# The expert stage of an attention and mixture-of-experts kernel with its tile loops written out

## The chip, the cores and the metric

The kernel runs on one core of a Trainium2 chip. The metric is the device time of one execution in microseconds (us). The engines are named as in the profile: PE (TensorE, matrix products), ACT (ScalarE), DVE (VectorE), POOL (GpSimd), SP (SyncE, which here only issues DMAs). Each engine runs its own instruction stream and meets the others only through semaphores.

## The reference, cut to what matters

The inputs are `x` and a context, each 128 sequences of 64 tokens of 128 numbers, 8192 tokens in all.

```python
x = x + xattn(layernorm(x), ctx, ctx)      # 16 heads of 64, causal, projected by Wo
z = layernorm(layernorm(x)) * ln_g + ln_b
w = top-2 of softmax(z @ rW + rb), renormalised          # 8 experts
hid = gelu(z @ W1[e] + b1[e])                            # 128 -> 256
mixed = sum over e of w[e] * (hid @ W2[e] + b2[e])       # 256 -> 128
return x + layernorm(x) + mixed
```

Each token goes to its two best experts only.

## The kernel before

**The attention stage**, up to about 754 us of the profiled execution, works through 16 groups of 512 tokens. PE, ACT, DVE, POOL and SP each run a hardware loop over groups. While it does group g it also routes the tokens of group g-1: DVE works out each token's two experts and a slot in the region of each, and POOL scatters the normalised rows to `slots` in DRAM by indirect DMA.

**The expert stage**, from about 754 to 1024 us, works through NT = 71 tiles of 256 slots. All slots of a tile belong to one expert, and which one is known only at run time: SP and DVE read the tile's row and expert from SBUF into a register (`value_load`). Buffers are DEEP = 4 deep, PSUM banks 2 deep. For one tile the engines do this:

- SP (`next_tile`, `load_tile`, lines 432 to 454): waits until tile s-4 has been transposed and its destinations are worked out, reads the row number, loads 256 rows of `slots` into `zin` (in the trace `kf<-slots`).
- PE (`rows_t` L1143, `up` L908 to L912, `down` L1161 and L1166): transposes tile s, multiplies tile s-1 by W1, tile s-2 by W2.
- ACT (`hi_part` L846, `results` L861, `hidden` L853): copies out the transposed rows of tile s, copies out the results of tile s-3 (`y_sb`, in the trace `kf<-bank`), applies Gelu to tile s-1.
- DVE (`lo_part` L1569, `expert_of` L1554, `places` L1586, `weights` L1560 to L1562, `destinations` L1575 and L1578): the low part of tile s, the indices `ix_i` to which the results of tile s-3 go, the weights of the expert of tile s+1 and its destinations.
- POOL (L704): two indirect DMAs for each tile scatter its results to `mixed` in DRAM. It waits for `ix_i` and `y_sb`, and its stream over all 71 tiles is written out in both kernels. The buffers `y_sb` and `ix_i` of tile s are free again when the scatters of tile s-4 have landed (`out_s`).

In the streams of the other four engines some of the tiles are written out one by one, and some are done in a loop whose body holds 4 tiles (SP, PE) or 8 (ACT, DVE). In a loop the tile's number is in a register, and a wait for a count that grows with the tile is a wait for a register's value, worked out by register instructions ahead of it. The loop's head is aligned (`head_slot`).

| engine | written out | in a loop | written out |
|---|---|---|---|
| SP | 0 to 23, 32 to 35 | 24 to 31 and 36 to 47 (2 and 3 rounds) | 48 to 70 |
| PE | 0 to 23 | 24 to 67 (11 rounds of 4) | 68 to 70 |
| ACT | 0 to 23 | 24 to 47 (3 rounds of 8) | 48 to 70 |
| DVE | 0 to 23 | 24 to 47 (3 rounds of 8) | 48 to 70 |

Beside tiles 0 to 23 stand the last group's routing and tables (DVE, PE, ACT), eight DMAs that pad the regions (`pad`, SP, L432 and L433, after tile 16), and beside tiles 54 to 70 the first ten groups are read back from `mixed`, scaled and added to `x` (`load_y`, `scale_second`, `add_experts`, `store`). The last six groups follow after the last tile.

Of the kernel before, what the change touches and what calls it, by code (L numbers as in the profile page):

```python
# [106 lines left out]
def xattn_ffn_kernel(nc, x, ctx_in, mask, Wq, Wk, Wv, Wo, bo, ln_g, ln_b, rW, rb, W1, b1, W2, b2, out):  # L107
# [8 lines left out]
    NG = NP // GP  # L116
# [4 lines left out]
    FG = 10  # L121
# [4 lines left out]
    FULL = -(-(2 * FG * TG - SPILL) // TILE)  # L126
# [11 lines left out]
    with ExitStack() as es:  # L138
# [116 lines left out]
        DEEP = 4  # L255
# [92 lines left out]
        def aligned_loop(engine, first, end):  # L348

            return nc.Fori(first, end, engines=[engine], head_slot={engine: 0})  # L350

        ROUTE = 23
        STRAIGHT = 24
        LOOPED = 48
        ADD_AT = dict(zip((54, 56, 58, 60, 62, 64, 66, 68, 69, 70), range(FG)))
        assert DONE <= LOOPED and len(ADD_AT) == FG and NT == 71

        def by_seq(par, b):
            return pr[par][:, :, :].rearrange("p (j b) s -> p j b s", b=2)[:, :, b, :]
# [26 lines left out]
        def _(sp):  # L386
# [54 lines left out]
            def rest_ready():  # L441

                sp.wait_ge(pad_ok, 16 * (1 + E))
                sp.wait_ge(sent, 32 * GP * NG)
                sp.wait_ge(tab, TAB_ALL)
# [6 lines left out]
            def next_tile(s, buf):  # L452
                sp.wait_ge(ct_ps, s - DEEP + 1)
                sp.wait_ge(yi_st, 2 * (s - DEEP) + 2)
                load_tile(s, buf)
# [17 lines left out]
            sp.wait_ge(sc_ps, 2 * (NP - 2))  # L473
            for s in range(DEEP):
                load_tile(s, s)
            for s in range(DEEP, STRAIGHT):
                next_tile(s, s % DEEP)
                if s == 16:
                    pad()
            with aligned_loop(mybir.EngineType.SP, STRAIGHT // DEEP, FULL // DEEP) as ss:  # L480
                for buf in range(DEEP):
                    next_tile(DEEP * ss + buf, buf)
            for s in range(FULL // DEEP * DEEP, FULL):
                next_tile(s, s % DEEP)
            rest_ready()
            for s in range(FULL, -(-FULL // DEEP) * DEEP):
                next_tile(s, s % DEEP)
            with aligned_loop(mybir.EngineType.SP, -(-FULL // DEEP), LOOPED // DEEP) as ss:
                for buf in range(DEEP):
                    next_tile(DEEP * ss + buf, buf)  # L490
            loaded = added = 0
            for s in range(LOOPED, NT):
                next_tile(s, s % DEEP)
                if s - 1 in ADD_AT:
                    if loaded == 0:
                        mixed_ready(DONE)
                    load_y(loaded)
                    loaded += 1
                if s - 5 in ADD_AT:
                    store(added)  # L500
                    added += 1
# [208 lines left out]
        def _(act):  # L710
# [131 lines left out]
            def hi_part(s, deep):  # L842
                act.wait_ge(ct_ps, s + 1)
                if not isinstance(s, int) or s >= DEEP:
                    act.wait_ge(up_ps, s - DEEP + 1)
                act.activation(z_hi[deep], bank[deep % 2][:, 0:TILE], ACT.Copy).then_inc(ch_hi, 1)  # L846

            def hidden(s, deep):
                act.wait_ge(up_ps, s + 1)
                if not isinstance(s, int) or s >= DEEP:  # L850
                    act.wait_ge(dn_ps, s - DEEP + 1)
                for c in range(FC):
                    act.activation(hid[deep][:, c, :], bank[2 + deep % 2][:, c * TILE:(c + 1) * TILE], ACT.Gelu,  # L853
                                   bias=w_f[deep][:, B1 + c:B1 + c + 1]).then_inc(gl_ok, 1)

            def results(s, deep):

                act.wait_ge(dn_ps, s + 1)
                if not isinstance(s, int) or s >= DEEP:
                    act.wait_ge(out_s[deep], 4 * TJ * (s - deep))  # L860
                act.activation(y_sb[deep], bank[4 + deep % 2][:, 0:TJ * D].rearrange("p (j d) -> p j d", d=D),  # L861
                               ACT.Copy).then_inc(yv_ok, 1)
# [13 lines left out]
                if s >= 1:  # L876
                    hidden(s - 1, (s - 1) % DEEP)

            for s in range(STRAIGHT):
                tile_out(s)  # L880
                if s == 4:
                    act.wait_ge(rz_ps, 1)
                    act.activation(z2T[:, :], bank[6][:, :], ACT.Copy).then_inc(rz_ok, 1)
                if s == 7:
                    r_exp(NG - 1)
            with aligned_loop(mybir.EngineType.Activation, STRAIGHT // (2 * DEEP), LOOPED // (2 * DEEP)) as ss:
                for k in range(2 * DEEP):
                    hi_part(2 * DEEP * ss + k, k % DEEP)
                    results(2 * DEEP * ss + k - 3, (k - 3) % DEEP)
                    hidden(2 * DEEP * ss + k - 1, (k - 1) % DEEP)  # L890
            act.wait_ge(rt_ok, ROUTE * NG)
            for s in range(LOOPED, NT):
                tile_out(s)
                if s in ADD_AT:
                    scale_second(ADD_AT[s])
            results(NT - 3, (NT - 3) % DEEP)
# [8 lines left out]
        def _(pe):  # L905
# [270 lines left out]
            rows_t(0, 0)  # L1176
            rows_t(1, 1)
            up(0, 0)
            for s in range(2, STRAIGHT):
                tile_products(s)  # L1180
                if s == 4:
                    pe.wait_ge(shifted, 2 * NP)
                    pe.wait_ge(zn_ok, GP * NG)
                    turned_rows(bank[6], zlast).then_inc(rz_ps, 1)
                if s == 5:
                    pe.wait_ge(att_ok, NP)
                    pe.wait_ge(rz_ok, 1)
                    logits(bank[7]).then_inc(rl_ps, 1)
                if s == 8:
                    pe.wait_ge(ch_ok, NG)  # L1190
                    ranks(bank[6]).then_inc(rx_ps, 1)
            with aligned_loop(mybir.EngineType.PE, STRAIGHT // DEEP, NT // DEEP) as ss:
                for k in range(DEEP):
                    rows_t(DEEP * ss + k, k)
                    up(DEEP * ss + k - 1, (k - 1) % DEEP)
                    down(DEEP * ss + k - 2, (k - 2) % DEEP)
            for s in range(NT // DEEP * DEEP, NT):
                tile_products(s)
            up(NT - 1, (NT - 1) % DEEP)
            down(NT - 2, (NT - 2) % DEEP)  # L1200
            down(NT - 1, (NT - 1) % DEEP)
# [3 lines left out]
        def _(dve):  # L1205
# [414 lines left out]
            weights(1, 1, expert_of(1))  # L1620
            add_attention(NP - 1)
            destinations(0, 0)
            for s in range(STRAIGHT):
                tile_in(s, s)
                if s == 0:
                    dve.wait_ge(att_ok, NP)
                    norm_stats(lambda t: xs[:, (NG - 1) * GP + t, :], norm[1], s1_ok, NG - 1)
                    twice_normed(NG - 1)
                if s == 1:
                    route_b(NG - 2)  # L1630
                if s == 2:
                    last_rows()
                if s == 6:
                    dve.wait_ge(rl_ps, 1)
                    route_a(NG - 1, bank[7], rl_ok, 1, zlast, first=True)
                if s == 9:
                    dve.wait_ge(rx_ps, 1)
                    route_c(NG - 1, bank[6], rx_ok, slot_ix_last)
                    dve.wait_ge(rx_ok, 1)
                    step(dve.tensor_copy(next_i[:, :], next_slot[:, :]))  # L1640
                    assert count[0] == TAB_NEXT
                if s == 10:
                    tiles_up(n_ceil[:, :], next_slot, 0)
                if s == 11:
                    step(dve.tensor_tensor(runs[:, 2, :], n_ceil[:, :], run_from[:, 2, :], ALU.subtract))
                    run_ends(2, 1)
                if s == 12:
                    later_ends()
                    step(dve.memset(run_row[:, RUNS:RUNS + 1], float(DEAD)))
                if s == 13:  # L1650
                    run_rows(1, 2)
                    run_jumps(RUNS)
                if s == 14:
                    route_b(NG - 1)
                if s == 15:
                    past_runs(REST, RUNS)
                if s == 16:
                    jumped_rows(REST, RUNS)
                if s == 18:
                    tile_experts(REST)  # L1660
                    assert count[0] == TAB_ALL
            with aligned_loop(mybir.EngineType.DVE, STRAIGHT // (2 * DEEP), LOOPED // (2 * DEEP)) as ss:
                for k in range(2 * DEEP):
                    tile_in(2 * DEEP * ss + k, k)
            dve.wait_ge(base_ok, NG)
            for s in range(LOOPED, NT):
                if s < NT - 1:
                    tile_in(s, s)
                else:
                    lo_part(s, s % DEEP)  # L1670
                    places(s - 3, (s - 3) % DEEP)
                if s in ADD_AT:
                    add_experts(ADD_AT[s])
# [31 lines left out]
```

## Time and profile before

| what | value |
|---|---|
| time, median of 3 runs | 1052.81 us (1048.83 to 1059.91) |
| the profiled execution | 1052.08 us |
| its span, first to last instruction | 1050.3 us |
| mean granted TensorE clock | 0.936 of full speed |
| busy: PE, DVE, ACT, POOL | 86%, 70%, 58%, 47% of the span |

The span is what the rows of the trace add up to; the 1.8 us between it and the execution's time lie before the first and after the last instruction. Shares are averages over stages: in the expert stage alone no engine is as busy as PE is in the attention stage. "Idle before" a row is the time in which its engine did nothing ahead of it, with who ended that. "Issue" means that the profile shows nothing that the engine waited for, and "remote", "another core or an unknown queue" that what released it came from none of the engines in the profile.

### The profile page before, as it was taken

The page shows a single profiled execution, that of the slowest core. Times are in us where ns is not written, and L with a number is a line of the kernel's source. Part 1 is how long each engine was busy: PE and PEld are TensorE (multiplying, and loading weights), DVE is VectorE, ACT ScalarE, POOL GpSimd, SP SyncE. Part 2 cuts the span into 40 slices and gives each one's busy share as a digit, 9 for nine tenths or more (in the row PEclk, how much of TensorE's full clock was granted, in tenths as well). Part 3 has the DMA queues.
Part 4 walks back from the last instruction along what each step waited for, and adds up shares of the span by engine and source line. Part 5 has one row for each costly group of instructions (what it writes and reads, how often), then busy time and mean ns, then how long its engine had stood idle before and what let it go on. Part 6 is the DMA issues. An engine that isn't in the chain of part 4 may idle for free.

```text
span 1050.3 us, 36518 instructions
## 1 busy us (share of the span) xinstructions
PE 900.1 (86%) x13368; PEld 784.9 (75%) x13368; DVE 731.1 (70%) x2239; ACT 611.7 (58%) x1317; POOL 489.0 (47%) x601
## 2 busy tenths in 40 slices
PE   8998999999999999999999999997776677777670
PEld 6887888887888888888888888886665566666560
DVE  6787877777777777777778787679366543445664
ACT  6675766766676676667567566665343343335462
POOL 2833543436454353644436364323356644555551
PEclk9999999999999999999999999999699678888895
DMA  9001010101001010110101000001123222224655
GB/s 283 20 22 31 15 35 8 35 8 38 29 11 35 5 35 11 34 30 10 36 5 35 28 18 23 8 17 28 36 62 103 81 75 69 72 80 138 190 164 197
DMA packets 55664, 56.63 MB, mean 54 GB/s; under 512 B 7335, under 2 KB 48593, under 8 KB 55601
## 3 DMA queue, kind: packets, MB, share of 16 engines
q1 hardware_dynamic: 46651, 37.94, 12.7%
q0 software_dynamic: 8640, 17.84, 5.1%
q8 instruction: 30, 0.49, 0.2%
q14 instruction: 33, 0.27, 0.1%
q10 hardware_dynamic: 310, 0.08, 0.1%
HBM read 32.62 MB, written 23.23 MB: 53 GB/s over the span
## 4 chain that ended last, share of the span: by engine, by line
PE 72%; issue 9%; another core or an unknown queue 6%; ACT 5%; DVE 4%; DMA 2%; SPq 1%; POOL 0%; DVEq 0%; ACTq 0%; POOLq 0%
PE bank L1023 11%; PE bank L908 10%; PE bank L912 10%; PE bank L909 9%; PE bank L1039 9%; PE bank L1008 7%; PE bank L991 5%; PE bank L1166 4%; ACT pr L853 2%; PE bank L961 1%; PE bank L936 1%; PE bank L1143 1%; DMA kf<-mixed 1%; PE bank L939 1%
## 5 line engine op out<-in xcount | busy, mean ns | idle before, releaser
L908 PE MATMUL bank<-in_h,Ah 128*128 128x256 f32 x654 | 212.6, 325 | 29.3 <-DVE Al L1569 16.3
L775 ACT ACTIVATE pr<-pr 128x512 f32<-128x512 f32 x128 | 80.4, 628 | 233.7 <-DVE pr L1281 233.7
L704 POOL DMA_INDIRECT mixed<-kf,ix_i x142 | 139.0, 979 | 115.7 <-DVE ix_i L1586 71.0
L728 ACT ACTIVATE kf<-bank 128x512 f32<-128x512 f32 x256 | 156.5, 612 | 8.0 <-PE bank L912 4.6
L908 PEld LDWEIGHTS bank<-in_h,Ah 128*128 128x128 f32 x654 | 128.6, 197 | 39.5 <-DVE Al L1569 19.0
L912 PE MATMUL bank<-in_h,Al 128*128 128x256 f32 x512 | 145.0, 283 | 0.0
L909 PE MATMUL bank<-in_l,Ah 128*128 128x256 f32 x512 | 144.6, 282 | 0.0
L615 POOL DMA_INDIRECT slots<-zrow,slot_ix x120 | 125.6, 1046 | 37.9 <-issue 28.3
L1279 DVE TENSOR_REDUCE mx<-bank 128x8 f32<-128x512 f32 x128 | 87.8, 686 | 76.0 <-PE bank L1039 75.8
L1023 PE MATMUL bank<-wo_s,oT 128*128 128x128 f32 x1024 | 134.8, 286 | 2.3 <-ACT oT L770 2.3
L550 POOL TENSOR_TENSOR idle_p<-half 128x1 f32<-128x1 f32 x114 | 27.5, 241 | 227.9 <-DVE slot_ix L1372 186.9
L1039 PEld LDWEIGHTS bank<-kf 64*64 64x64 f32 x4096 | 82.7, 136 | 66.8 <-issue 65.7
L1039 PE MATMUL bank<-kf 64*64 64x64 f32 x4096 | 103.4, 227 | 31.2 <-issue 30.1
L1166 PE MATMUL bank<-kf,pr 128*128 128x128 f32 x568 | 95.7, 319 | 39.2 <-ACT pr L853 35.1
L1023 PEld LDWEIGHTS bank<-wo_s,oT 128*128 128x128 f32 x1024 | 122.4, 196 | 6.9 <-ACT oT L770 2.7
L1291 DVE TENSOR_TENSOR pr<-pr,ri 128x512 f32<-128x512 f32 x128 | 115.4, 902 | 4.4
L1166 PEld LDWEIGHTS bank<-kf,pr 128*128 128x128 f32 x568 | 81.0, 220 | 50.0 <-ACT pr L853 37.5
L853 ACT ACTIVATE pr<-bank,kf 128x256 f32<-128x256 f32 x142 | 59.8, 477 | 76.5 <-remote 53.2
L555 POOL TENSOR_TENSOR rs<-ve,half 128x4 f32<-128x4 f32 (+1 forms) x32 | 43.7, 1366 | 125.7 <-DVE ve L1220 100.4
L909 PEld LDWEIGHTS bank<-in_l,Ah 128*128 128x128 f32 x512 | 98.0, 191 | 0.0
L912 PEld LDWEIGHTS bank<-in_h,Al 128*128 128x128 f32 x512 | 97.2, 190 | 0.0
L1281 DVE TENSOR_TENSOR pr<-bank,mx 128x512 f32<-128x512 f32 x128 | 88.5, 692 | 4.4
(191 smaller groups left out, 1955.6 us busy)
## 6 DMA issues: line engine op xcount, KB each, us to landing
kf<-slots SPq DMA_DIRECT2D x71, 130.0 KB
kf<-mixed SPq DMA_DIRECT2D x12, 512.0 KB
xs<-in_x_dram SPq DMA_DIRECT2D x16, 256.0 KB
c_in<-in_ctx_dram SPq DMA_DIRECT2D x16, 256.0 KB
out_dram<-xs SPq DMA_DIRECT2D x16, 256.0 KB
mixed<-kf,ix_i POOLq DMA_INDIRECT x142
vf<-mixed SPq DMA_DIRECT2D x4, 512.0 KB
slots<-zrow,slot_ix POOLq DMA_INDIRECT x120
```

The costliest lines, as they stand in the source:

```text
L615: pool.indirect_dma_start(out=slots, out_offset=bass.IndirectOffsetOnAxis(ap=ix[:, k, t:t + 1], axis=0), in_=rows[:, t, :], in_offset=None ...
L704: pool.indirect_dma_start(out=mixed, out_offset=bass.IndirectOffsetOnAxis(ap=ix_i[buf][:, j:j + 1], axis=0), in_=y_sb[buf][:, j, :], in_of ...
L728: act.activation(kfs[par][:, 2 * u:2 * u + 2, :], ring[gr.bank(name)].rearrange("p (h t) -> p h t", h=2), ACT.Copy).then_inc(act_ev, 1)
L908: pe.matmul(ps, lh, rh, start=True, stop=False)
L909: pe.matmul(ps, lh, rl, start=False, stop=False)
L912: return pe.matmul(ps, ll, rh, start=False, stop=True)
L1023: last = pe.matmul(o_ps[:, 0:D], oT[:, j, :], wo_s[:, j, :], start=(j == 0), stop=(j == H // 2 - 1))
L1039: last = pe.matmul(s_ps[b][place, S * j:S * j + S], kfs[par][dims, j, toks], kfs[par][dims, H // 2 + j, toks], start=False, stop=True, ski ...
L1166: last = pe.matmul(into[:, j, :], hid[deep][:, c, j * P:(j + 1) * P], w_f[deep][:, c * D:(c + 1) * D], start=False, stop=(c == FC - 1), sk ...
L1279: dve.reduce_max(mx[:, par, hs], src, AX_X).then_inc(sm_st, 1)
L1281: dve.tensor_tensor(by_seq(par, t), src, mx[:, par, hs].unsqueeze(2).to_broadcast([P, 8, S]), ALU.subtract).then_inc(shifted, 1)
L1291: dve.tensor_tensor(by_seq(par, t), by_seq(par, t), ri[:, par, hs].unsqueeze(2).to_broadcast([P, 8, S]), ALU.mult).then_inc(probs, 1)
```

## The change

The loops are gone. On SP, PE, ACT and DVE each tile from 24 on is written out as the first 24 and the last 23 were: the tile's number is a constant, each wait is for a constant, and buffer addresses are constants. The row and the expert of a tile are still read from SBUF into a register by each of SP and DVE. The order of the work on each engine is the same, with two places where it is now a condition in one long loop of the program text: `rest_ready` on SP still comes ahead of tile 33, and ACT's wait for `rt_ok` still comes after tile 47, now behind the work of tile 48 instead of ahead of it. PE's whole stream of 71 tiles is written out, DVE waits for `base_ok` ahead of tile 48 as before. The attention stage's loops stay.

```diff
@@ SP
-            for s in range(DEEP, STRAIGHT):
+            for s in range(DEEP, ADD_FROM):
+                if s == FULL:
+                    rest_ready()
                 next_tile(s, s % DEEP)
                 if s == 16:
                     pad()
-            with aligned_loop(mybir.EngineType.SP, STRAIGHT // DEEP, FULL // DEEP) as ss:
-                for buf in range(DEEP):
-                    next_tile(DEEP * ss + buf, buf)
...
-            with aligned_loop(mybir.EngineType.SP, -(-FULL // DEEP), LOOPED // DEEP) as ss:
-                for buf in range(DEEP):
-                    next_tile(DEEP * ss + buf, buf)
@@ ACT
-            for s in range(STRAIGHT):
+            for s in range(NT):
                 tile_out(s)
...
-            with aligned_loop(mybir.EngineType.Activation, STRAIGHT // (2 * DEEP), LOOPED // (2 * DEEP)) as ss:
-                for k in range(2 * DEEP):
-                    hi_part(2 * DEEP * ss + k, k % DEEP)
-                    results(2 * DEEP * ss + k - 3, (k - 3) % DEEP)
-                    hidden(2 * DEEP * ss + k - 1, (k - 1) % DEEP)
-            act.wait_ge(rt_ok, ROUTE * NG)
-            for s in range(LOOPED, NT):
-                tile_out(s)
+                if s == ADD_FROM:
+                    act.wait_ge(rt_ok, ROUTE * NG)
@@ PE
-            for s in range(2, STRAIGHT):
+            for s in range(2, NT):
                 tile_products(s)
...
-            with aligned_loop(mybir.EngineType.PE, STRAIGHT // DEEP, NT // DEEP) as ss:
-                for k in range(DEEP):
-                    rows_t(DEEP * ss + k, k)
-                    up(DEEP * ss + k - 1, (k - 1) % DEEP)
-                    down(DEEP * ss + k - 2, (k - 2) % DEEP)
@@ DVE
-            for s in range(STRAIGHT):
+            for s in range(ADD_FROM):
                 tile_in(s, s)
...
-            with aligned_loop(mybir.EngineType.DVE, STRAIGHT // (2 * DEEP), LOOPED // (2 * DEEP)) as ss:
-                for k in range(2 * DEEP):
-                    tile_in(2 * DEEP * ss + k, k)
```

## Rows read from the trace of the kernel before

**Rows 1.** Busy time by stretch; columns: the stretch, then each engine, PEclk the granted clock.
```profile
core 0: us, PE busy (x) PEld busy (x) DVE busy (x) ACT busy (x) POOL busy (x), PEclk, DMA share, GB/s
849.00:935.00 86.00, 65.25 (x408) 56.50 (x407) 38.51 (x161) 32.65 (x92) 45.31 (x47) 0.84 0.25 73
935.00:957.00 22.00, 16.88 (x103) 14.57 (x102) 9.94 (x44) 9.81 (x28) 10.25 (x11) 0.84 0.30 91
```
**Rows 2.** Timeline of ACT, start and length in us: `hi_part` of tiles 17, 24, 48, 54, 70.
```profile
825.62 0.38 ACT L846 ACTIVATE in_h<-bank 128x256 fp32r<-128x256 f32 x1
...
850.88 0.38 ACT L846 ACTIVATE in_h<-bank 128x256 fp32r<-128x256 f32 x1 [2.67 <-PE bank L912]
...
936.69 0.40 ACT L846 ACTIVATE in_h<-bank 128x256 fp32r<-128x256 f32 x1
...
957.58 0.38 ACT L846 ACTIVATE in_h<-bank 128x256 fp32r<-128x256 f32 x1 [0.68 <-PE bank L1143]
...
1018.79 0.38 ACT L846 ACTIVATE in_h<-bank 128x256 fp32r<-128x256 f32 x1 [2.51 <-remote]
```
**Rows 3.** Groups by line, busy and idle before: 850.8 to 936.6 us, then 936.6 to 957.5.
```profile
L846 ACT ACTIVATE in_h<-bank 128x256 fp32r<-128x256 f32 x24 | 9.3, 387 | 22.3 <-PE bank L1143 7.8 <-PE bank L912 5.6 <-issue 4.5
...
L846 ACT ACTIVATE in_h<-bank 128x256 fp32r<-128x256 f32 x6 | 2.3, 390 | 5.5 <-remote 2.6 <-PE bank L1143 1.7 <-issue 1.2
```
**Rows 4.** Timeline of POOL, looped tiles: a run of six scatters and the next run's first.
```profile
893.81 0.97 POOL L704 DMA_INDIRECT mixed<-kf,ix_i  x1 [2.65 <-DVE ix_i L1586]
...
900.14 0.96 POOL L704 DMA_INDIRECT mixed<-kf,ix_i  x1 [0.30 <-issue]
904.99 0.97 POOL L704 DMA_INDIRECT mixed<-kf,ix_i  x1 [3.90 <-DVE ix_i L1586]
```
**Rows 5.** Timeline of ACT beside that run.
```profile
896.21 0.38 ACT L861 ACTIVATE kf<-bank 128x256 f32<-128x256 f32 x1
902.43 0.84 ACT L853 ACTIVATE pr<-bank,kf 128x256 f32<-128x256 f32 x2 [5.84 <-remote]
```
**Rows 6.** Timeline of POOL and ACT, written-out tiles: first and last scatter of a run of six.
```profile
987.73 0.96 POOL L704 DMA_INDIRECT mixed<-kf,ix_i  x1 [1.66 <-DVE ix_i L1586]
...
994.33 0.96 POOL L704 DMA_INDIRECT mixed<-kf,ix_i  x1 [0.30 <-issue]
...
990.36 0.39 ACT L861 ACTIVATE kf<-bank 128x256 f32<-128x256 f32 x1
996.42 0.84 ACT L853 ACTIVATE pr<-bank,kf 128x256 f32<-128x256 f32 x2 [5.67 <-remote]
```
**Rows 7.** Waits, 849 to 935 us (loops): total us, times, longest.
```profile
POOL mixed L704 <- DVE ix_i L1586: 28.6, 10, 3.9
...
ACT pr L853 <- remote: 22.1, 5, 5.8
...
DVE ix_i L1586 <- issue: 11.7, 23, 0.8
```
**Rows 8.** Waits, 935 to 957 us (written out but for PE).
```profile
ACT pr L853 <- remote: 4.7, 1, 4.7
...
DVE ix_i L1586 <- issue: 2.3, 7, 0.5
```
**Rows 9.** Instruction packets (count, MB): 797 to 849 us, then 851 to 935.
```profile
q8 instruction: 2, 0.03, 0.3%
q14 instruction: 5, 0.04, 0.2%
...
q14 instruction: 3, 0.02, 0.1%
```
**Rows 10.** Waits of PE over the whole span: a wait in the attention stage.
```profile
PE bank L936 <- issue: 3.5, 4, 2.9
```
**Rows 11.** The chain that ended last, 790 to 812 us: start, us, what.
```profile
796.40 0.71 SPq L432
...
797.86 0.70 SPq L433
```

More of the change, by code:

```diff
@@ L352, in xattn_ffn_kernel @@
         ROUTE = 23
-        STRAIGHT = 24
-        LOOPED = 48
+        ADD_FROM = 48
         ADD_AT = dict(zip((54, 56, 58, 60, 62, 64, 66, 68, 69, 70), range(FG)))
-        assert DONE <= LOOPED and len(ADD_AT) == FG and NT == 71
+        assert DONE <= ADD_FROM and len(ADD_AT) == FG and NT == 71
         def by_seq(par, b):
@@ L479, in _ @@
                     pad()
-            with aligned_loop(mybir.EngineType.SP, STRAIGHT // DEEP, FULL // DEEP) as ss:
-                for buf in range(DEEP):
-                    next_tile(DEEP * ss + buf, buf)
[L483 to L487, printed above, removed]
-            with aligned_loop(mybir.EngineType.SP, -(-FULL // DEEP), LOOPED // DEEP) as ss:
-                for buf in range(DEEP):
-                    next_tile(DEEP * ss + buf, buf)
             loaded = added = 0
-            for s in range(LOOPED, NT):
+            for s in range(ADD_FROM, NT):
                 next_tile(s, s % DEEP)
@@ L885, in _ @@
                     r_exp(NG - 1)
-            with aligned_loop(mybir.EngineType.Activation, STRAIGHT // (2 * DEEP), LOOPED // (2 * DEEP)) as ss:
-                for k in range(2 * DEEP):
-                    hi_part(2 * DEEP * ss + k, k % DEEP)
-                    results(2 * DEEP * ss + k - 3, (k - 3) % DEEP)
-                    hidden(2 * DEEP * ss + k - 1, (k - 1) % DEEP)
-            act.wait_ge(rt_ok, ROUTE * NG)
-            for s in range(LOOPED, NT):
-                tile_out(s)
+                if s == ADD_FROM:
+                    act.wait_ge(rt_ok, ROUTE * NG)
                 if s in ADD_AT:
@@ L1191, in _ @@
                     ranks(bank[6]).then_inc(rx_ps, 1)
-            with aligned_loop(mybir.EngineType.PE, STRAIGHT // DEEP, NT // DEEP) as ss:
-                for k in range(DEEP):
-                    rows_t(DEEP * ss + k, k)
-                    up(DEEP * ss + k - 1, (k - 1) % DEEP)
-                    down(DEEP * ss + k - 2, (k - 2) % DEEP)
-            for s in range(NT // DEEP * DEEP, NT):
-                tile_products(s)
             up(NT - 1, (NT - 1) % DEEP)
@@ L1661, in _ @@
                     assert count[0] == TAB_ALL
-            with aligned_loop(mybir.EngineType.DVE, STRAIGHT // (2 * DEEP), LOOPED // (2 * DEEP)) as ss:
-                for k in range(2 * DEEP):
-                    tile_in(2 * DEEP * ss + k, k)
             dve.wait_ge(base_ok, NG)
-            for s in range(LOOPED, NT):
+            for s in range(ADD_FROM, NT):
                 if s < NT - 1:
```

## The prediction

> **What bounds the kernel now.** I read the busy time by stretch first, to see whether an engine fills the part that the change touches. None does: over the looped tiles PE is busy 65.25 of 86 us, POOL 45.31, DVE 38.51, ACT 32.65, and over the first tiles behind the loops PE has 16.88 of 22 us, much the same share [rows 1]. So the stage is bounded by waits, and the next view is the timeline, for the pace. Tile 24 to tile 48 is 936.69 - 850.88 = 85.81 us for 24 tiles, 3.58 us a tile [rows 2, 3]. PE, the busiest engine, has 65.25 / 24 = 2.7 us of work in each, with a mean granted clock of 0.84 [rows 1], so 0.9 us or more of every tile is waiting.
>
> Where does it wait? POOL's timeline shows it. POOL works in runs: six scatters back to back from 893.81 to 901.10, one every 1.27 us, which is 2.53 us a tile, then nothing until 904.99 [rows 4]. ACT stops inside such a run: its last copy ends at 896.59, 2.8 us after the run's start, and the next Gelu starts at 902.43, 1.3 us after the run's end, released by something "remote" [rows 5]. PE then has no Gelu output, and DVE no high part. Once ACT goes on, the pipeline has to refill before POOL gets its next indices, which is the 3.90 us on its next row [rows 4]. This repeats, with runs mostly of six and of four scatters. Why ACT stops I can't say from the trace. Its awaited matrix product was done, and no wait of its program at that place is for a DMA. What I can say is that it goes with POOL's runs, and POOL's stream is not changed.
>
> The decisive view is the same pair of timelines where ACT, DVE and SP are already written out. POOL has a run of six from 987.73 to 995.29, ACT stops at 990.75, 3.0 us after its start, and goes on at 996.42, 1.1 us after its end, with an idle time of 5.67 us beside 5.84 us in the loop [rows 5, 6]. The pause doesn't know whether the code around it is a loop.
>
> **The change part by part.** *Register instructions and register waits, all four engines.* They are removed for tiles 24 to 47 (PE: to 67). Most run ahead of the engine's work and are hidden by it. The before kernel holds its own experiment: the same work at both kinds of code. Written out, tiles 48 to 54 take 957.58 - 936.69 = 20.89 us, 3.48 us a tile [rows 2, 3]; tiles 17 to 24, written out on ACT, DVE and PE, take 850.88 - 825.62 = 25.26 us for 7, 3.61 us a tile [rows 2]. Against the loop's 3.58 this gives 24 x (3.48 - 3.58) = -2.2 us at one end, 24 x (3.61 - 3.58) = +0.8 us at the other. Since both short stretches are one or two rounds of the run-and-pause rhythm, each is uncertain by a few tenths of a microsecond a tile. A second way to size it from below: the one place where I can see register instructions on the path is DVE's idle time ahead of L1586, with "issue" as its cause, 11.7 us in 23, 0.51 us each in the loop, and 2.3 us in 7, 0.33 us each written out [rows 7, 8]. It counts only when POOL stands waiting for `ix_i`, 10 times in the looped stretch [rows 7]: 10 x 0.18 = -1.8 us. The two agree, and I take -2 us. I cost the rest of the removed register work at nothing: its cover is the wait for the pause's end, or PE's products. If that cover were gone, the 23 gaps would all count, 23 x 0.18 = -4.1 us, the lower end.
>
> *Loop branches and the aligned heads.* These are 11 rounds on PE, 5 on SP and 3 each on ACT and DVE, 22 in all. ACT's first tile in the loop starts after 2.67 us of idling [rows 2]. That is a pause of the usual kind, so the entry costs between nothing and 2.7 us, once; I take nothing, the pauses being what ends it. For the other branches I have no row that shows a wait, and take nothing.
>
> The Trainium skill has a rule here (Runtime: NRT & Kernel Launch, section Instruction fetch mechanics): a taken branch whose target isn't among the two pages held makes the engine stand until the page is fetched, and kernels prefer to be unrolled for it. For the loops of this stage the trace speaks against its applying: PE's instruction queue, q8, moves no packet from 851 to 935 us, while PE goes round its loop, and q14 moves three [rows 9]. The same skill (Advanced Engine Details and Errata, section Control Flow Timing) has some 108 ns for a compare-and-branch, by which 22 of them would be 2.4 us if all lay on the path; no row here times one.
>
> *Instructions to be fetched.* This is what the change adds. In 52 us of written-out code (797 to 849) there are 2 packets on q8 and 5 on q14; in 84 us of looped code 0 and 3 [rows 9]. Carried over, tiles 24 to 47 get some 3 more on q8 and 5 more on q14, and PE's tiles 48 to 67 another 3: about 11 pages. Hidden, they cost nothing; the pace of tiles 17 to 24 and 48 to 54 holds such fetches already and is the loop's. Unhidden, the nearest row is the longest wait of PE with no cause shown, 2.9 us, at its entry into the attention loop [rows 10]. The bounds are 0 and 11 x 2.9 = 32 us; I take 0, since the written-out stretches are the same code and therefore the nearest rows.
>
> *Order and waits.* No wait is added. ACT's wait for `rt_ok` moves behind tile 48's work, and that count was reached some thirty tiles before: nothing either way. SP's `rest_ready` stays ahead of tile 33. SP's loads run about three tiles ahead of PE; fewer register instructions there move none of them onto the path. The tail behind the last tile and the attention stage aren't touched.
>
> The sum, against the profiled execution's own 1052.08 us: 1052.1 - 2 = 1050 us. That execution is 0.7 us from the median of the three runs, which spread over 11 us, so the same 1050 stands for the median, and a difference of 1%, 10.5 us, is about what a measurement of this kernel can tell from no change.
>
> **The rivals.** *The pauses shrink (faster).* During pauses the register and DMA instructions of SP take 0.70 us each [rows 11]. If the pauses are made by the number of such instructions that the engines issue together, fewer of them would mean shorter pauses. The loops' pauses on ACT's Gelu are 22.1 us in 86 [rows 7]. With four in ten of that gone, 9 us, and the 2 us above, the time is 1041. Against it: written out, the same wait is 4.7 us in 22 [rows 8], 0.21 us per us against the loops' 0.26. For it: that small difference has the right sign.
>
> *The fetches are not hidden (slower).* PE and ACT run their written-out streams through pages that must come by DMA, while loads and scatters use the same DMA engines. If 6 of the 11 new pages cost their 2.9 us [rows 10], that is +17 us, 1067 with the 2 us gained. It decides from four such waits on (4 x 2.9 = 11.6, past 1%). For it: the written-out stretch from 797 to 849 is the slowest of the stage, but its chain runs through SP's eight padding DMAs [rows 11], which explain that. Against it: the pace of tiles 48 to 54.
>
> *The branches did cost (much faster).* If PE's 11 loop rounds each held a wait like the 2.9 us one, the time would be 1052.1 - 32 = 1020. The absence of q8 packets in the looped stretch makes it the least likely. This is the skill's rule on branches, turned into a time by the trace's own row.
>
> *That the change does nothing* is nearly my forecast, and its time, 1052, lies within it.
>
> **How the numbers follow.** The forecast, no change or a gain of a few microseconds at an unchanged rhythm, has 0.73. The shrinking pauses have 0.12, the branches 0.03, the unhidden fetches 0.12. Faster by over 1% is then 0.12 + 0.03 = 0.15, slower by over 1% 0.12, within 1% 0.73. The time is the forecast's, 1050. Its own range is 1045 to 1057: -4.1 - 2.7 us and +0.8 us about 1052, widened by the spread of the runs. The range for 8 in 10 reaches into both neighbours, to a part of the pause rival's gain (1040) and to three exposed fetches (1052 + 9 = 1061).
>
> **What would show it.** In the changed kernel's timeline the 24 tiles from 24 to 48 should take 82 to 87 us; ACT's pauses with a "remote" release should still come inside POOL's runs of four and six, up to 5.8 us long; DVE's issue gap ahead of L1586 should be 0.33 us rather than 0.51 in this stretch. The instruction queues should show some ten packets more after 850 us, with no new idle time beside them. I am wrong if PE or ACT has new waits of 2 to 3 us with "issue" as cause next to an instruction packet, or if POOL's runs become shorter and the pauses with them, or if the stretch between 850 and 937 us moves by more than 5 us in either direction.

## The result and the profile after

The changed kernel took 1048.14 us (median of 20 runs, 1043.85 to 1054.01) beside 1052.93 us for the kernel before (20 runs, 1048.83 to 1059.91): a ratio of 0.9963, 95% interval 0.9945 to 0.9981, which is 3.9 us less (the two medians differ by 4.8 us). The forecast was 1050 us.

That holds for the occasion on which the pair was timed. The kernels of an experiment were timed side by side in sets, and the sets came out in two kinds. In one kind the kernel before takes 1045.8 to 1052.9 us and its trace has the pauses of ACT that the prediction describes. In the other kind it takes 924.8 to 925.0 us, has no such pauses, and the change gives nothing that can be told from noise. They are called the long sets and the short sets below, and ratios are always within one set. What makes a set long or short is not known. It need not be the chip: the results of both short sets and of one of the two long ones carry chip number 7, the other long one number 6, and whether a number always means the same chip is not known. The pair above is of the long kind.

The stretch that answers to [rows 1] in the changed kernel, busy time by stretch:

```profile
852.00:936.00 84.00, 63.32 (x423) 54.23 (x421) 38.75 (x170) 34.67 (x97) 47.89 (x50) 0.92 0.28 80
```

PE is still busy three quarters of it, so the stage is still bounded by waits. PE's granted clock is 0.92 here beside 0.84 before [rows 1], which is taken up with the table below. The timeline of ACT gives the pace, as in [rows 2], with `hi_part` of tiles 17, 24, 48, 54 and 70:

```profile
828.82 0.38 ACT L836 ACTIVATE in_h<-bank 128x256 fp32r<-128x256 f32 x1
...
853.26 0.38 ACT L836 ACTIVATE in_h<-bank 128x256 fp32r<-128x256 f32 x1 [1.20 <-PE bank L1127]
...
936.65 0.38 ACT L836 ACTIVATE in_h<-bank 128x256 fp32r<-128x256 f32 x1 [0.74 <-remote]
...
957.51 0.38 ACT L836 ACTIVATE in_h<-bank 128x256 fp32r<-128x256 f32 x1 [0.69 <-remote]
...
1011.91 0.38 ACT L836 ACTIVATE in_h<-bank 128x256 fp32r<-128x256 f32 x1
```

Tiles 24 to 48 take 936.65 - 853.26 = 83.4 us instead of 85.8, about the 2 us that were forecast. But tiles 54 to 70 take 54.4 us instead of 61.2 [rows 2], and beside those only PE's code differs.

The pause is still there. First POOL's timeline of the changed kernel, for [rows 4], then ACT's, for [rows 5]:

```profile
900.93 0.96 POOL L694 DMA_INDIRECT mixed<-kf,ix_i  x1 [2.28 <-DVE ix_i L1563]
...
907.34 0.96 POOL L694 DMA_INDIRECT mixed<-kf,ix_i  x1 [0.30 <-issue]
911.25 0.96 POOL L694 DMA_INDIRECT mixed<-kf,ix_i  x1 [2.96 <-DVE ix_i L1563]
```

```profile
903.29 0.38 ACT L851 ACTIVATE kf<-bank 128x256 f32<-128x256 f32 x1
908.84 0.84 ACT L843 ACTIVATE pr<-bank,kf 128x256 f32<-128x256 f32 x2 [5.17 <-remote]
```

A run of six scatters, ACT stopped 2.7 us after its start and going on 0.5 us after its end; POOL then stands for 2.96 us where it stood for 3.90. Waits of the changed kernel, 852 to 938 us (total us, times, longest), for [rows 7]:

```profile
ACT pr L843 <- remote: 19.8, 5, 5.2
POOL mixed L694 <- DVE ix_i L1563: 19.5, 8, 3.0
...
DVE ix_i L1563 <- issue: 8.1, 25, 0.6
```

POOL's wait for its indices fell from 28.6 to 19.5 us, and DVE's issue gap from 0.51 to 8.1 / 25 = 0.32 us. Instruction packets in the same stretch, for [rows 9]:

```profile
q8 instruction: 3, 0.05, 0.3%
q14 instruction: 7, 0.06, 0.2%
```

3 and 7 packets where the loops had 0 and 3. Over the whole execution the page has five more on q8, 35 for 30, and the 33 of before on q14:

```profile
q8 instruction: 35, 0.57, 0.2%
q14 instruction: 33, 0.27, 0.1%
```

PE's longest waits with no cause shown, 850 to 1025 us, are nonetheless about what they were (4.1 us in 2, longest 3.1, in the kernel before; on the products of `up` 3.9 us in 4 for 2.9 us in 3):

```profile
PE bank L1150 <- issue: 4.5, 2, 3.2
```

### The profile page after: what moved, and what is told of

It is laid out like the page before. It is cut to its first block, busy times and chain, and to the rows that moved or that the text cites. A ratio compares the mean times of both kernels' runs of the same rounds, so it can differ in the third digit from the quotient of the medians.

```text
span 1044.1 us, 36120 instructions
## 1 busy us (share of the span) xinstructions
PE 903.5 (87%) x13368; PEld 786.9 (75%) x13368; DVE 731.6 (70%) x2238; ACT 612.8 (59%) x1317; POOL 488.2 (47%) x601
## 4 chain that ended last, share of the span: by engine, by line
PE 71%; DVE 9%; issue 8%; another core or an unknown queue 5%; ACT 4%; DMA 1%; DVEq 0%; POOL 0%; POOLq 0%; SPq 0%; ACTq 0%
PE bank L1007 11%; PE bank L892 10%; PE bank L896 9%; PE bank L893 9%; PE bank L1023 9%; PE bank L992 7%; PE bank L1150 5%; PE bank L975 5%; PE bank L945 1%; PE bank L1127 1%; PE bank L920 1%; DVE Al L1546 1%; ACT pr L843 1%; DVE pr L1268 1%
## 5 line engine op out<-in xcount | busy, mean ns | idle before, releaser
L605 POOL DMA_INDIRECT slots<-zrow,slot_ix x120 | 126.2, 1052 | 38.0 <-issue 28.3
L1007 PE MATMUL bank<-wo_s,oT 128*128 128x128 f32 x1024 | 137.4, 290 | 2.3 <-ACT oT L760 2.3
L1007 PEld LDWEIGHTS bank<-wo_s,oT 128*128 128x128 f32 x1024 | 124.8, 199 | 6.9 <-ACT oT L760 2.7
L1268 DVE TENSOR_TENSOR pr<-pr,ri 128x512 f32<-128x512 f32 x128 | 118.7, 928 | 4.4
L843 ACT ACTIVATE pr<-bank,kf 128x256 f32<-128x256 f32 x142 | 59.7, 475 | 66.1 <-remote 39.5
```

Source lines behind the costliest of these rows:

```text
L605: pool.indirect_dma_start(out=slots, out_offset=bass.IndirectOffsetOnAxis(ap=ix[:, k, t:t + 1], axis=0), in_=rows[:, t, :], in_offset=None ...
L1007: last = pe.matmul(o_ps[:, 0:D], oT[:, j, :], wo_s[:, j, :], start=(j == 0), stop=(j == H // 2 - 1))
L1268: dve.tensor_tensor(by_seq(par, t), by_seq(par, t), ri[:, par, hs].unsqueeze(2).to_broadcast([P, 8, S]), ALU.mult).then_inc(probs, 1)
```

## The experiments

There are four sets. The first and the third came out short, the second and the fourth long, by chance. Their chip numbers are 7, 6, 7 and 7.

**The changed kernel again** (no edit).

> The changed kernel once more, as the control of this set. Both theories: a ratio of 0.994 to 0.998 against the kernel before (0.9963 measured). What I look at is the split: theory A (the gain is the fewer register instructions of DVE, ACT and SP beside tiles 24 to 48) expects 82 to 84.5 us for tiles 24 to 48 again and, since nothing but PE differs there, 57 to 61 us for tiles 54 to 70, so that the 54.4 us of the first profile was chance. Theory B (PE's written-out tiles 48 to 67 give the gain) expects 54 to 56 us for tiles 54 to 70 again.

Measured in a short set: 925.24 us beside 924.82, ratio 1.0013 (0.9994 to 1.0033). Both theories were wrong about the ratio, since neither knew of such a case.

**The kernel before again** (no edit), beside it.

> The kernel before against itself: how far two profiles of one kernel differ in each stretch. Ratio 0.998 to 1.002. If tiles 54 to 70 take under 58 us here (61.2 in the first profile), the stretch is a matter of chance in every kernel and theory B has no ground; if they take 60 to 62 us again, theory B stands.

Measured: 924.19 us, ratio 0.9995 (0.997 to 1.0019). Its waits, 745 to 890 us:

```profile
ACT kf L861 <- DMA mixed<-kf,ix_i: 40.8, 33, 4.2
POOL mixed L704 <- issue: 28.7, 94, 0.3
DVE ix_i L1586 <- DMA mixed<-kf,ix_i: 20.1, 24, 2.4
```

No wait of ACT from tile 0 to tile 70 is released by something "remote". POOL goes from one scatter to the next in 0.3 us, 104 times on end, and ACT and DVE wait until a scatter has landed and their buffer is free. In a short set the stage is bounded by POOL's scatters:

```profile
789.45 0.95 POOL L704 DMA_INDIRECT mixed<-kf,ix_i  x1 [0.30 <-issue]
...
793.38 0.96 POOL L704 DMA_INDIRECT mixed<-kf,ix_i  x1 [0.30 <-issue]
794.64 0.95 POOL L704 DMA_INDIRECT mixed<-kf,ix_i  x1 [0.30 <-issue]
```

That is 1.26 us for most scatters, and with the few longer ones 59.6 / 24 = 2.5 us a tile from tile 24 to 48. Whatever makes ACT, PE or DVE quicker should be lost there.

**All but PE.** SP, ACT and DVE written out, PE's loop kept.

```diff
-            for s in range(2, NT):
+            for s in range(2, STRAIGHT):
                 tile_products(s)
...
+            with aligned_loop(mybir.EngineType.PE, STRAIGHT // DEEP, NT // DEEP) as ss:
+                for k in range(DEEP):
+                    rows_t(DEEP * ss + k, k)
+                    up(DEEP * ss + k - 1, (k - 1) % DEEP)
+                    down(DEEP * ss + k - 2, (k - 2) % DEEP)
+            for s in range(NT // DEEP * DEEP, NT):
+                tile_products(s)
```

> SP, ACT and DVE written out, PE's loop over tiles 24 to 67 kept. Theory A: all of the gain is here, 1048 us, ratio 0.995 to 0.998, tiles 24 to 48 in 82 to 84.5 us. Theory B: at most 1 us of the gain, ratio 0.998 to 1.001, tiles 54 to 70 in 60 to 62 us as before.

Short set: 926.47 us, ratio 1.0016 (0.9994 to 1.0038).

**PE alone.** The other half: the diff of the change for PE, and nothing else.

> PE alone written out, the loops of SP, ACT and DVE kept. Theory A: PE's register instructions and branches are hidden, so nothing, ratio 0.999 to 1.001, tiles 24 to 48 in 85 to 86.5 us. Theory B: most of the gain, ratio 0.995 to 0.998, tiles 54 to 70 in 54 to 56 us.

Short set: 923.76 us, ratio 0.9975 (0.9952 to 0.9999). With the pauses absent, neither half decides between theory A and theory B, though PE alone has its interval just below 1.

**A third run of the changed kernel** opened the second set, a long one.

> The changed kernel a third time, as the control of this set. The set before showed a chip on which both kernels take 925 us and ACT's pauses are absent. Theory C: the gain exists only where the pauses exist, because only there does POOL stand idle and wait for DVE's indices. It expects a ratio of 0.994 to 0.998 if the kernel before takes about 1050 us on this chip, and 0.999 to 1.003 if it takes about 925 us. Theory D, that the gain has nothing to do with pauses and the set before was a chance, expects 0.994 to 0.998 on either.

Measured: 1040.99 us beside 1045.84, ratio 0.9948 (0.9931 to 0.9965). Theory D falls with the 1.0013 of the short set, and theory C's main claim stands: the gain is there where the pauses are.

**Places first.** DVE hands POOL its indices before it reads the next tile's expert.

```diff
                 fresh = not isinstance(s, int) or s >= 1
-                e = expert_of(s + 1) if fresh else None
                 if not isinstance(s, int) or s >= 3:
                     places(s - 3, (k - 3) % DEEP)
+                e = expert_of(s + 1) if fresh else None
```

> The changed kernel, with DVE's read of the next tile's expert moved behind the instruction that hands POOL its indices (L1563), instead of ahead of it. Theory C on a chip of about 1050 us: POOL gets its indices some 0.3 to 0.45 us earlier at each of some 25 refills, 7 to 11 us faster than the changed kernel, 1037 to 1042 us. On a chip of about 925 us: POOL never waits for the indices beside tiles 12 to 60, so within 1 us of the changed kernel. The rival, that the weights of the next tile are then late for PE, expects 1 to 3 us more than the changed kernel on both.

Measured: 1037.23 us, ratio 0.9921 (0.9896 to 0.9947), 3.8 us less than the changed kernel of the same set by the medians. The two intervals overlap a little, so that it is the fastest of all is likely and not shown, and the size is half of what I expected. DVE's issue gap ahead of the indices is gone from its waits, and yet POOL waits for them nearly as long over the whole stage, 757 to 1025 us. The first row is the changed kernel's third run, the second is places first:

```profile
POOL mixed L694 <- DVE ix_i L1563: 55.7, 24, 4.0
```

```profile
POOL mixed L694 <- DVE ix_i L1563: 53.8, 25, 4.2
```

A link that was 0.36 us shorter in each of 25 refills took 1.9 us from this wait, not 9. In tiles 24 to 70 alone, which the table below compares, it took 4.6 us (40.2 to 35.6). One profile of each can't settle it further: the two profiled executions took nearly the same time, 1036.84 and 1036.70 us, so the 3.8 us between the medians isn't in this pair. What is shown is that the gain stays below the 9 us that the shortened link would give by itself.

**DVE alone** written out, the change's diff for DVE and nothing else.

> DVE alone written out. Theory C on a chip of about 1050 us: DVE's shorter way to the indices is the gain beside tiles 24 to 48, ratio 0.996 to 0.999, tiles 24 to 48 in 83 to 85 us. On a chip of about 925 us: nothing or slower, ratio 1.000 to 1.003, and if it is DVE that disturbs POOL's scatters there, they have a mean of 1.03 us or more beside tiles 24 to 36 as in the changed kernel, and not 0.98 as in the kernel before.

Measured in the long set: 1043.98 us, ratio 0.9983 (0.9964 to 1.0001), with 84.6 us for tiles 24 to 48. Both lie where theory C had them, but the interval also holds no gain at all; it may be a part of the gain or nothing.

**One scatter.** POOL scatters one half of each tile's results; the other half is left out.

```diff
-                for j in range(TJ):
+                for j in range(1):
                     pool.indirect_dma_start(
...
-                    act.wait_ge(out_s[deep], 4 * TJ * (s - deep))
+                    act.wait_ge(out_s[deep], 4 * (s - deep))
...
             load_next(group_of(NG - 2), NG - 2, last=True)
+            sp.wait_ge(ld_w[3], 16)
+            for g in range(NG):
+                sp.dma_start(mixed[g * 2 * TG:(g + 1) * 2 * TG, :].rearrange("(p a) d -> p a d", p=P),
+                             wo_s[:, :, :]).then_inc(filled, 16)
+            sp.wait_ge(filled, 16 * NG)
```

(and the two other waits for `out_s`, on DVE and SP, in the same way)

> The changed kernel with one scatter for each tile instead of two. The second half of each tile's results is left out, and mixed is filled with other numbers at the end of the attention stage by sixteen plain DMAs, which the first load of the expert stage waits for. Theory C: POOL's runs are the cause of the pauses on a chip of about 1050 us and the bound on one of about 925 us, so the pauses shrink to under 2 us each, and tiles 24 to 48 take 55 to 62 us on either, PE's own pace. The rival, that something else stops ACT, expects pauses of 4 us or more to stay on a chip of about 1050 us and 75 us or more for these tiles.

Measured in the long set: 969.93 us, one run. The pauses are gone but for one of 3.0 us near the stage's start, and tiles 24 to 48 take 53.4 us, under the 55 to 62 expected, with a granted clock of 1.00. Its POOL timeline, one row for each tile:

```profile
848.05 0.96 POOL L700 DMA_INDIRECT mixed<-kf,ix_i  x1 [1.26 <-DVE ix_i L1569]
850.28 0.97 POOL L700 DMA_INDIRECT mixed<-kf,ix_i  x1 [1.26 <-DVE ix_i L1569]
852.50 0.96 POOL L700 DMA_INDIRECT mixed<-kf,ix_i  x1 [1.25 <-DVE ix_i L1569]
```

A tile takes 2.22 us, steadily, and the waits of ACT's Gelu, 757 to 940 us, hold one "remote":

```profile
ACT pr L849 <- remote: 3.0, 1, 3.0
```

This settles the largest point: without half of POOL's scatters the pauses of a long set are gone, and with them over 1 us a tile. The experiment takes away several things at once, the number of scatters, the bytes that they write and their coming back to back, and it doesn't tell these apart. Nor are runs enough by themselves: in a short set POOL makes runs of over a hundred scatters and ACT has no pause.

**All but PE and PE alone, second time**, for the answer of a long set.

> SP, ACT and DVE written out, PE's loop kept, once more, for a chip of about 1050 us. Theory C1 (the gain comes from the three engines on the way from a pause's end to POOL's next indices): ratio 0.995 to 0.998, and tiles 24 to 48 in 82 to 84 us. Theory C2 (PE's written-out tiles give half or more of it): ratio 0.998 to 1.000, tiles 54 to 70 in 58 to 61 us. On a chip of about 925 us both expect 1.000 to 1.003.

> PE alone written out, once more, for a chip of about 1050 us. Theory C1: ratio 0.999 to 1.001, tiles 24 to 48 in 85 to 87 us. Theory C2: 0.995 to 0.998, tiles 54 to 70 in 52 to 56 us. On a chip of about 925 us both expect 0.996 to 1.000, as measured there.

A short set again. All but PE: 927.14 us, ratio 1.0026 (1.0004 to 1.0048). PE alone: 925.18 us, ratio 0.9994 (0.9968 to 1.002).

**All but PE, third time**, and **the kernel before** beside it.

> SP, ACT and DVE written out, PE's loop kept, a third try to have it on a chip of about 1050 us. Theory C1: ratio 0.995 to 0.998 and tiles 24 to 48 in 82 to 84 us. Theory C2 (half or more of the gain is PE's): 0.998 to 1.000, tiles 54 to 70 in 58 to 61 us. On a chip of about 925 us: 1.001 to 1.004, as measured there.

> The kernel before against itself beside it: how far a second profile differs by stretch. On a chip of about 1050 us I expect tiles 24 to 48 in 85 to 87 us; tiles 54 to 70 in 60 to 62 us if the 61.2 of the first profile is the kernel's, and under 58 if it was chance. On a chip of about 925 us: 59 to 61 and 47 to 49 us, as measured there.

A long set. All but PE: 1052.53 us beside 1051.97, ratio 1.001 (0.999 to 1.0031). The kernel before against itself: 1053.03 us, 1.0013 (0.9984 to 1.0042). Without PE's part the gain is absent: the interval doesn't touch that of either measurement of the whole change in a long set, though the whole change was not timed in this one. Theory C1, which had been mine from the prediction on, falls. Tiles 54 to 70 take 57.8 us, just under the 58 to 61 of theory C2; in the kernel before they take 54.9 us, under 58, so that by the measure set beforehand the 61.2 us of the first profile was chance, and these tiles alone say nothing for PE. The waits of all but PE, 850 to 1025 us:

```profile
ACT pr L845 <- remote: 52.3, 10, 5.9
...
DVE ix_i L1572 <- issue: 13.6, 42, 0.8
ACT in_h L838 <- remote: 8.4, 3, 3.0
```

and the same of the changed kernel:

```profile
ACT pr L843 <- remote: 24.7, 7, 5.2
DVE ix_i L1563 <- issue: 15.2, 41, 1.1
ACT in_h L836 <- remote: 13.0, 10, 3.6
```

DVE's gap is as short in the one as in the other, 0.32 and 0.37 us. The pauses are 60.7 us in all with PE's loop and 37.7 without, but this window is fixed and the tiles in it differ, so the table counts each kernel from its tile 24 to its tile 70. It puts together, for all profiles, the stretches (differences of ACT's `hi_part` starts, us), the pauses (both "remote" rows), POOL's wait for `ix_i` from DVE, and the mean granted clock.

| kernel, long sets | 24 to 48 | 48 to 54 | 54 to 70 | 24 to 70 | pauses | longest | POOL's wait | clock |
|---|---|---|---|---|---|---|---|---|
| before | 85.8 | 20.9 | 61.2 | 167.9 | 50.5 | 5.8 | 48.4 | 0.85 |
| before again | 89.2 | 22.0 | 54.9 | 166.1 | 35.7 | 6.1 | 49.9 | 0.86 |
| all but PE | 89.0 | 21.1 | 57.8 | 167.9 | 55.6 | 5.9 | 54.1 | 0.86 |
| DVE alone | 84.6 | 23.8 | 55.8 | 164.2 | 48.7 | 5.8 | 48.8 | 0.88 |
| changed | 83.4 | 20.9 | 54.4 | 158.6 | 37.7 | 5.2 | 40.4 | 0.86 |
| changed, third run | 82.3 | 20.6 | 52.1 | 155.0 | 37.1 | 4.4 | 40.2 | 0.91 |
| places first | 77.4 | 20.2 | 59.1 | 156.7 | 39.5 | 4.4 | 35.6 | 0.92 |
| one scatter | 53.4 | 13.4 | 44.5 | 111.3 | 0 | | | 1.00 |

| kernel, short sets | 24 to 48 | 48 to 54 | 54 to 70 | 24 to 70 |
|---|---|---|---|---|
| before again | 59.6 | 16.3 | 48.2 | 124.1 |
| PE alone, twice | 59.6, 60.7 | 16.1, 15.8 | 47.5, 47.7 | 123.2, 124.3 |
| changed | 65.9 | 15.6 | 47.5 | 129.0 |
| all but PE, twice | 65.0, 65.2 | 16.4, 16.3 | 48.4, 49.0 | 129.8, 130.6 |

In the long sets the four profiles with PE's loop need 164.2 to 167.9 us for tiles 24 to 70; the three with PE written out need 155.0 to 158.6. POOL's wait for its indices divides them in the same way, 48.4 to 54.1 us against 35.6 to 40.4, and so does the longest pause. The sum of the pauses does not: the kernel before has 35.7 us of them in its second profile, less than any kernel with PE written out. Two profiles of the kernel before differ by 6.3 us in tiles 54 to 70 and by 3.4 the other way in 24 to 48: a stretch of a few pauses says little, their sum says more. And each row is one execution, up to 4 us from its kernel's median (all but PE 1056.28 for 1052.53, the changed kernel's third run 1036.84 for 1040.99), so the table overstates the gain.

The granted clock is a rival that no run separates. In tiles 24 to 48 it is 0.84 to 0.87 in the four with PE's loop and 0.89 to 0.92 in the three without, and it may be what the shorter time comes from or what comes of it. It can't be the whole: over tiles 24 to 70 the changed kernel's first profile has 0.86, as the second of the kernel before, and takes 7.5 us less.

## Why the prediction was right, and where not

**The time** was right: 1048.14 us lies within the forecast's own 1045 to 1057 us. The sign was right too, and the size, 0.2% forecast and 0.37% measured, about half. That a gain this small came out at all for the reason given is not shown, and in part it was luck, as the third point says.

**What bounds the kernel** was right for a long set. ACT's pauses go with POOL's scatters; taking away half of the scatters took the pauses away and brought a tile to 2.22 us. It was said in general, though, and holds for one kind of set. In the other the same program is bounded by the scatters themselves.

**The term for the register instructions** was half of what was measured and is not shown to have the right cause, and this is the step that failed: "The two agree, and I take -2 us". One of the two ways was the pace of written-out tiles, the other DVE's shorter issue gap at 10 refills. DVE's gap did shrink as forecast, 0.51 to 0.32 us. But it shrank as much in all but PE, whose ratio is 1.001 (0.999 to 1.0031, so at most 1 us of gain). DVE alone, at 0.9983 (0.9964 to 1.0001), would allow the 1.8 us, if ACT's and SP's written-out tiles cost 1 us or more; no run shows it. Their agreement was chance: the pace was read from 6 and 7 tiles, and the two profiles of the kernel before differ by 1.1 us in tiles 48 to 54 (20.9 and 22.0), by 3.4 us in tiles 24 to 48.

**"I cost the rest of the removed register work at nothing: its cover is the wait for the pause's end, or PE's products."** For PE this is the second fault. The view that the prediction calls decisive, [rows 6], lies in tiles where ACT, DVE and SP are written out but PE is still in its loop, so it could say nothing about PE's code, and the measured gain is absent without PE's part. PE's stream has 252 register, branch and wait instructions between 850 and 1025 us in the kernel before, and 93, all of them waits, in the changed one, by the trace. What they lengthen is not shown. The saved time stands in POOL's wait for its indices, 8 to 10 us less in the changed kernel than in the kernel before; but POOL's own work is the same, so it had to stand there, whatever the cause. My rival of the shrinking pauses, given 0.12, isn't borne out as it stood: the longest pause is shorter, 4.4 to 5.2 us for 5.8 to 6.1, but the sum of the pauses is not lower than in the second profile of the kernel before, where the rival had 9 us gone from the loops alone. I had looked for the instructions on SP, which were visible at 0.70 us each, and not on PE.

**Order, branches, fetches.** Right, as far as the traces go: I had estimated some 11 packets more and the page has 5, all on PE's queue (35 in every trace with PE written out, 30 in every one with PE's loop), with no new wait of 2 to 3 us beside them, and in the short sets PE alone was at 0.9975 and 0.9994. The fetch rival is refuted for PE. The Trainium skill's rule (Runtime: NRT & Kernel Launch, section Instruction fetch mechanics) that a straight stream's pages are mostly fetched out of sight agrees with this: five packets more, and no loss. Its rule on taken branches finds no case in the loops, where PE's queue moved no packet from 851 to 935 us [rows 9]; the rival of the branches, 1020 us, is far from the 1048 measured.

**What stays open.** Whether PE's written-out tiles give the gain alone or only together with the other engines': PE alone was run in both short sets and in no long one. In what way PE's instructions cost time, and what part of the gain is the granted clock. Why the written-out SP, ACT and DVE cost 4 to 6 us in tiles 24 to 48 in a short set. About half of that is only moved there: tiles 0 to 24, whose code is the same, take 69.8 to 70.1 us in these kernels and 71.6 to 73.0 in the others, and by the ratios the whole kernel loses 1.2 to 2.4 us. There, POOL's scatters are longer beside them; groups by line, 757 to 825 us, first the changed kernel, then the kernel before:

```profile
L694 POOL DMA_INDIRECT mixed<-kf,ix_i x50 | 53.4, 1068 | 15.2 <-issue 14.9 <-ACT kf L851 0.3
```

```profile
L704 POOL DMA_INDIRECT mixed<-kf,ix_i x53 | 52.7, 993 | 16.2 <-issue 14.6 <-DVE ix_i L1586 1.2 <-ACT kf L861 0.3
```

The 0.075 us on each scatter would be 2 x 24 x 0.075 = 3.6 us of those 4 to 6, an estimate from these two rows; all but PE has 1050 and 1056 ns and PE alone 1006 and 990 ns in the same window. So POOL's scatters are longer where the three engines are written out. DVE alone was meant to show whether it is DVE, and it came in a long set. And what makes a set long or short is not known either.

## What to carry to other kernels

Where an engine's stream pauses at a fixed phase of another engine's runs, look for the cause in those runs and change them: here half of the scatters were worth 71 us (one run), and all loops together 4. A view that leaves one engine's code as it was can't price a change to that engine. Before sizing a gain by one link of a chain, shorten that link alone; two estimates that agree at 2 us prove nothing when one kernel's two profiles differ by 6 us in a stretch. When profiles are compared, count from the same tile to the same tile, not in a fixed window. And time a small gain on more than one occasion, with the kernel before beside it each time, since it may exist on one kind alone.

## What the hardware showed that I had not expected

One program takes 925 us in one set and 1052 in another, with the same durations of single instructions (the scatter's 0.96 us, ACT's copies of L728 614 and 612 ns). The time up to the first tile's `hi_part` is 694.6 against 754.5 us, the rest 229.9 against 295.8 us. The granted clock doesn't account for the first part: from 50 to 690 us it is 0.99 in the short one and 1.00 in the long one.

In a long set PE's updates of semaphores are recorded late during a run of scatters. These are the recorded updates beside the pause of [rows 5], read from the trace of the kernel before, in us, with the semaphore's name in the program:

```
dn_ps 895.39   ct_ps 895.90   ...   up_ps 902.40   dn_ps 902.54   ct_ps 902.58   up_ps 902.66
```

and the last landings of POOL's scatters (`out_s[2]`) are at 902.19, 902.34 and 902.37. PE had started the products that belong to the updates after 902 between 895.3 and 898.3, and by their modelled ends all were done by 898.6. DVE's updates came meanwhile without delay: one at 898.39, when its cast of L1560 ended at 898.38, and one at 899.09, when L1575 ended at 899.08. So by the trace ACT was idle not for want of a product, but for want of the news of it, which came within 0.03 us of the scatters' last landing. That rests on modelled ends: the trace doesn't show when a product was really written. In the short set, in the kernel before, each of the 71 updates of `dn_ps` comes within 0.015 us of its product's modelled end; in the long set's first profile 26 of the 66 that are recorded come more than 0.1 us after it. With one scatter for each tile, in a long set too, 37 of the 39 recorded are within 0.015 us again. A release so long after its product would also be why the profile calls the releaser "remote".
